# Lattice stage: the sine product moves to VectorE and all eight rows of the normalisation to GpSimd

## What is computed

```
scores = einsum("bhqd,bhkd->bhqk", q, k) / 8
i = int(abs(scores) * 1618);  scores = where(i % 9 in (0, 3, 6), scores / PHI, scores)
attn = softmax(scores)
attn = attn * (sin(C1 * attn) * exp(-attn**2 / PHI) + cos(C2 * attn))
ctx  = einsum("bhqk,bhkd->bhqd", attn, v)
```

## Time and profile before

| | before |
|---|---|
| median of 3 runs | 5878.8 us (5863.97 to 5885.81) |
| the profiled execution | 5868.64 us, of it 5866.9 us span |
| PE busy | 4792.8 us (82%) |
| DVE busy | 4141.1 us (71%) |
| ACT busy | 3988.8 us (68%) |
| POOL busy | 3773.1 us (64%) |
| mean granted TensorE clock | 0.944 of full speed |

### The profile page before, as it was taken

How to read it: one execution, slowest core, us unless ns; L and a number is a source line. 1 busy time by engine, 2 the same in 40 slices (tenths; PEclk the granted TensorE clock), 3 DMA queues, 4 the chain that set the end, 5 groups by cost and what they waited for, 6 DMA issues and landing times. The chain is left out here.

```text
span 5866.9 us, 98280 instructions
## 1 busy us (share of the span) xinstructions
PE 4792.8 (82%) x27646; PEld 2698.8 (46%) x27689; DVE 4141.1 (71%) x7553; ACT 3988.8 (68%) x5466; POOL 3773.1 (64%) x3599
## 2 busy tenths in 40 slices
PE   2688888888888888888888888888888869997899
PEld 1344444444444444444444444444444436554566
DVE  2577777777777777777777777777777656665664
ACT  1577777777777777777777777777777734444332
POOL 4577777777777777777777777777777634443233
PEclk9799999999999999999999999999999879999999
DMA  0000000000000000000000000000000000000000
GB/s 5 23 9 8 8 8 8 8 9 8 10 8 8 8 8 8 8 8 8 9 8 10 8 8 8 8 8 8 8 9 8 4 9 1 2 2 15 3 6 7
DMA packets 34184, 45.24 MB, mean 8 GB/s; under 512 B 24521, under 2 KB 24585, under 8 KB 34058
## 3 DMA queue, kind: packets, MB, share of 16 engines
q1 hardware_dynamic: 32010, 43.49, 2.8%
q0 software_dynamic: 2048, 0.14, 0.1%
HBM read 39.40 MB, written 4.19 MB: 7 GB/s over the span
## 5 line engine op out<-in xcount | busy, mean ns | idle before, releaser
L588 PE MATMUL banks<-ident,att 128*128 128x128 f32 x8192 | 1148.2, 287 | 410.0 <-DVE ag L520 252.1
L588 PEld LDWEIGHTS banks<-ident,att 128*128 128x128 f32 x8192 | 944.6, 147 | 1004.1 <-DVE ag L520 616.9
L630 PE MATMUL banks<-kT,qT 128*128 128x512 f32 x2048 | 1144.8, 658 | 278.9 <-DVE mx L549 269.6
L390 POOL TENSOR_TENSOR sinb<-sinb,ag 128x1024 f32<-128x1024 f32 x512 | 1281.5, 2506 | 85.4 <-ACT sinb L461 70.4
L540 DVE SCALAR_TENSOR_TENSOR mag<-near,mag 128x512 f32<-128x512 int32 x1024 | 857.7, 842 | 483.6 <-POOL near L406 474.2
L400 POOL TENSOR_SCALAR mag<-mag 128x512 f32<-128x512 f32 x1024 | 689.5, 678 | 573.1 <-DVE mag L540 539.0
L647 PE MATMUL outp<-sinb,vo 128*64 128x512 f32 x2048 | 1046.3, 636 | 0.0
L647 PE MATMUL outp<-work,vo 128*64 128x512 f32 x2048 | 1046.3, 636 | 0.0
L406 POOL TENSOR_SCALAR near<-mag 128x512 int32<-128x512 f32 x1024 | 794.0, 775 | 363.9 <-ACT mag L479 300.3
L479 ACT ACTIVATE mag<-banks 128x512 f32<-128x512 f32 x1024 | 599.2, 592 | 283.1 <-PE banks L630 283.0
L497 DVE TENSOR_TENSOR work<-banks,work 128x1024 f32<-128x1024 f32 x512 | 625.1, 1221 | 192.8 <-ACT work L455 189.8
(11 more groups left out here) (198 smaller groups left out, 6357.7 us busy)
## 6 DMA issues: line engine op xcount, KB each, us to landing
x<-xT_dram SPq DMA_DIRECT2D x128, 256.0 KB, 3.5
xT_dram<-xT SPq DMA_DIRECT2D x8, 256.0 KB, 2.9
out<-hres SPq DMA_DIRECT2D x8, 256.0 KB, 2.6
base<-in_L_tok_turns,idx POOLq DMA_INDIRECT x64, 2.3
wqk<-in_L_attn_Wq SPq DMA_DIRECT2D x64, 16.0 KB
wqk<-in_L_attn_Wk SPq DMA_DIRECT2D x64, 16.0 KB
wqk<-in_L_attn_bq SPq DMA_DIRECT2D x64, 0.2 KB
wqk<-in_L_attn_bk SPq DMA_DIRECT2D x64, 0.2 KB
```

Of the source, the lines that this page charges most:

```text
L390: nc.gpsimd.tensor_tensor(sinb[:, k % RING], sinb[:, k % RING], ag[:, k], ALU.mult).then_inc(tmul, 1)
L588: mm = nc.tensor.matmul(turn_pair(k)[:, c, i * P:(i + 1) * P], att[:, p, 4 * half + i, kt * P:(kt + 1) * P], ident[:], is_transpose=True, ...
L630: nc.tensor.matmul(score_bank(n), qT[:, p, (n // 2) * P:(n // 2 + 1) * P], kT[:, p, (n % 2) * 512:(n % 2 + 1) * 512], start=True, stop=Tru ...
```

## The change

The multiplication of sine and gauss term (*product*) is taken from GpSimd's queue and issued by VectorE, behind the turns of the same step and before its keeps and filters. Rows 3 and 7 of the normalisation are taken from VectorE, so GpSimd normalises all eight. The second counter `weights2` goes, and the waits on it: turns and fills now wait for `weights` alone. Tiles, sizes, the step of every operation, ScalarE's and TensorE's queues stay as they are.

```diff
-        DVE_ROWS = (TB // 2 - 1, TB - 1)
@@ gpsimd
-                        if a - P3 in SINE:
-                            k = SINE.index(a - P3)
-                            wait(pool, sined, TB * g + k + 1)
-                            wait(pool, agd, TB * (g + 1))
-                            nc.gpsimd.tensor_tensor(sinb[:, k % RING], sinb[:, k % RING], ag[:, k],
-                                                    ALU.mult).then_inc(tmul, 1)
-                        if a - NORM in EXP and EXP.index(a - NORM) not in DVE_ROWS:
+                        if a - NORM in EXP:
                             j = EXP.index(a - NORM)
                             held(pool, recip, TB * g + j + 1)
                             nc.gpsimd.tensor_scalar(att[:, p, j], att[:, p, j], rs[:, j:j + 1], TURN,
@@ vector
-                        if a - NORM in EXP and EXP.index(a - NORM) in DVE_ROWS:
-                            j = EXP.index(a - NORM)
-                            wait(dve, recip, TB * g + j + 1)
-                            nc.vector.tensor_scalar(att[:, p, j], att[:, p, j], rs[:, j:j + 1], TURN,
-                                                    ALU.mult, ALU.mult).then_inc(weights2, 1)
                         if a - TURNS in EXP:
                             j = EXP.index(a - TURNS)
-                            if j in DVE_ROWS:
-                                wait(dve, weights2, 2 * g + j // 4 + 1)
-                            else:
-                                wait(dve, weights, (TB - 2) * g + j + 1 - j // 4)
                             wait(dve, nned, TB * g)
+                            wait(dve, weights, TB * g + j + 1)
                             nc.vector.tensor_scalar(nturn[:, j], att[:, p, j], ROUND, -ROUND,
                                                     ALU.add, ALU.add).then_inc(turned, 1)
+                        if a - P3 in SINE:
+                            k = SINE.index(a - P3)
+                            wait(dve, sined, TB * g + k + 1)
+                            wait(dve, agd, TB * (g + 1))
+                            nc.vector.tensor_tensor(sinb[:, k % RING], sinb[:, k % RING], ag[:, k],
+                                                    ALU.mult).then_inc(tmul, 1)
@@ tensor, fill
-                wait(pe, weights, (TB - 2) * g + (TB // 2 - 1) * (half + 1))
-                wait(pe, weights2, 2 * g + half + 1)
+                wait(pe, weights, TB * g + TB // 2 * (half + 1))
```

## The result

The changed kernel takes 5881.6 us (median of 20 runs, 5864.0 to 5903.0) against 5859.3 us for the kernel before (20 runs beside it, 5847.7 to 5889.8). The ratio is 1.0037, 95% interval 1.0026 to 1.0049: slower by 0.4%. I had forecast 0.3% faster. Both lie inside "within 0.5%", but the sign is wrong, and there lies the lesson of this case.

The account below looks back on a forecast made before the run. No engine's total sets the time; TensorE, then GpSimd with VectorE, then ScalarE bound each head in turn. Terms 2.35 - 1.15 - 0.9 give 0.3 us a head, 0.25 rounded, 18 us in all: 5861 us, range 5830 to 5895.

Parts of the forecast that it names:

- Parts 1 and 2: Product moves from GpSimd to VectorE at about 1.2 us each; turns 0 starts earlier, gaining 2.35 us a head.
- the walk: Reading one head's engine queues in order of time to price the change: 0.3 us gained a head, 0.25 with rounding.
- (b): Stretch from remove 7 to the first gauss product; TensorE has gaps, GpSimd runs without one, then trades tiles with VectorE.
- Rival A's first half: VectorE's product does not keep GpSimd out, gaining 1.1 us before filter 0; rival A's chance as a whole 0.30.
- Muls 4 and 7 just in time: Before removes 4 and 7: mul 4 ends at 2109.9, mul 7 at 2120.8, both just in time, at no cost.
- Rival B: Products ahead of keep and mul on VectorE make muls 4 and 7 late: 20 to 60 us slower, chance 0.18.
- (a): Stretch from remove 0 to remove 7, where TensorE works nearly without a gap.
- the sum: The terms of one head added: 2.35 - 1.15 - 0.9 = 0.3 us gained, 0.25 with rounding.
- Part 3: Norm 3 on GpSimd: keep 3 comes 7.8 us after turns 0 instead of 6.65, costing 1.15 us a head.
- Part 4: Norm 7 on GpSimd takes 1.62 us and delays fill 4 and ScalarE's square, costing 0.9 us a head.
- (c): Stretch from the first gauss product to the next head's remove 0; ScalarE is full from fill 4's square on.
- Rival C: Lower clock level falls into stretch (a) of every head: 35 us slower, 5896 us, chance 0.08.

Follow-up runs that it names:

- split: Changed kernel with norms 3 and 7 back on VectorE, so only the product moves: 5744.7 us, ratio 0.9809 to the kernel before.
- norm7_lean: lean with norm 7 back on VectorE, norm 3 left on GpSimd: 5792.8 us, ratio 0.9885 to the kernel before.
- split_lean: split with the same waits left out as in lean: 5746.7 us, ratio 0.9807 to the kernel before.
- norms_pool: Kernel before with all eight norms on GpSimd and the product still there: 6057.5 us, ratio 1.0337.
- norm3_lean: lean with norm 3 back on VectorE, norm 7 left on GpSimd: 5851.2 us, ratio 0.9982 to the kernel before.
- lean: Changed kernel with 14 waits a head left out that the first of their kind already covers: 5852.2 us, ratio 0.9991 to the kernel before.
- warm4p: Changed kernel with score 4 done four times and the projection ahead of fill 4 three times: 5845.4 us, ratio 0.997 to the kernel before.

## Why the prediction was right and wrong, step by step

**Parts 1 and 2, gain 2.35 us: right.** Turns 0 starts 7.24 us behind remove 7 on average (7.48 in the heads without the wait at mul 7), where the walk gave 7.3 and the kernel before has 9.7; alone (split) the move takes 2.53 us out of (b), about 2.2 in the heads without that wait. The product's price of 1.2 us was 1.23. The exclusion of the two engines, on which the walk rests, is there with the new product too:

```profile
2054.94 1.67 POOL L399 TENSOR_SCALAR near<-mag 128x512 int32<-128x512 f32 x1 [3.89 <-ACT mag L472]
2057.45 1.50 POOL L399 TENSOR_SCALAR near<-mag 128x512 int32<-128x512 f32 x1 [0.84 <-DVE mag L531]
```

Against these two rounds stand VectorE's products 6 and 7, started at 2054.92 and 2057.25 for 1.22 us each; a round without one takes 0.62 us. Rival A's first half is refuted: VectorE's product does keep GpSimd out. The trace agrees with the rule weighed in the prediction (the Trainium skill, "SBUF — State Buffer", "Who interferes with whom"). So the engines do not meet only at semaphores, as was said at the start: these two also hold each other up without one.

**Muls 4 and 7 just in time: right, with one exception.** Rival B did not come: stretch (a) is not longer at full clock (23.73 against 23.95 us); that it became 0.2 us shorter is in none of the sum's terms. The exception is that remove 7 comes 0.8 us late in every second head, by the wait at mul 7 and not by the product; (b) gives 0.5 us of it back, which leaves 0.1 us a head.

**Part 3, norm 3, cost 1.15 us: right.** It measures 1.12 us from norm7_lean against split_lean, and 1.11 from norms_pool against before.

**Part 4, norm 7, cost 0.9 us: right for the order of work, wrong for what it set off.** Norm 7 took 1.61 us, where the walk gave 1.62, and fill 4 waited for GpSimd 1.97 us in one head and 3.40 us in another; at full clock (c) grew from 23.94 to 24.90 us, 0.96. But the mean (c) grew by 2.18 us, from 24.25 to 26.43: the other 1.2 is the lower level behind fill 4, to which the sum gave nothing. The row of norm 7:

```profile
2082.43 1.61 POOL L388 TENSOR_SCALAR att<-att,rs 128x1024 f32<-128x1024 f32 x1
```

**Rival C, the clock, is the step that failed.** I gave it 0.08 and saw it in one place only: I asked whether the lower level would fall into stretch (a) of every head, as it did of every second one. I did say that the gap before fill 0 would grow from 2.5 to 3.9 us (it grew to 3.49). I did not ask the same of the gap before fill 4, which the walk itself had made 1.2 us longer, nor what lay behind it: matmuls that feed ScalarE at the beginning of its full stretch. There the lower level came, in 42 heads of 62, at 1.3 to 2.9 us each. In the whole head it costs 1.9 us in place of 0.9. The 0.6 us that the new order gains is less than this 1.0 and the 0.1 of the wait at mul 7, and the head is 0.5 us longer: 33 us over 63 heads, less 6 us around them, is the 27 us between the two profiled executions. C's time of 5896 us is by chance that of the profiled execution; its mechanism is right, its place and its chance were wrong. The forecast of 5861 us also stood on 10.2 us between the profiled execution and the median of three runs; with 20 runs the median of before lies 9 us below that execution.

In one sentence: all terms of the sum in the order of work were within about 0.2 us of what was measured, and the term that I had left as a rival was larger than their sum.

**What is shown, and what is not.** Shown: that the lower level falls on fill 4 and scores 7 and 8 in after and that (c) of 42 of 62 heads is over 1 us longer than at full clock, all of them with the lower level in it, where before has 6 such heads and norm7_lean none; and that with norm 7 on GpSimd it lies in (c) whoever does the product (after, norm3_lean, norms_pool). It is no plain rule: lean, with norm 7 on GpSimd, has 19 such heads, and split and split_lean, with it on VectorE, have 17 and 13. Shown too: that filling TensorE's gaps gives time back in after and none in before. Not settled: what decides in which of the heads it comes, and why the wait at mul 7 is 1.6 to 1.9 us in norm7_lean and norm3_lean and 0.4 to 0.9 in the others that have it. In lean 19 heads have it and in after 42, for a difference of 14 waits a head; and most edits that kept it from one place brought some of it to another. I have seen where it falls; a rule for it I haven't.

## What to carry to other kernels

Walk the queues for a change in the order of work, and the terms came out to about 0.2 us here; then ask of every gap of TensorE that the walk makes longer what stands right behind it. If that feeds an engine that is full from there on, price it once at full clock and once at the lower level, and give the second a real chance: here it cost 1.0 us a head against a gain of 0.6. Take a change of several moves apart: the product's move alone was worth 1.9%, and the two norms that came with it cost all of that and more. And before a longer stretch is put down to the clock, look at the granted clock of that very stretch and at the instruction packets: two runs here had a stretch (a) that was 1.8 us longer in every second head at full clock.

## What was not expected of the hardware

- **The lower clock level is a shifting cost.** It was made less in these runs and partly moved, never removed: the mean granted clock went from 0.938 (after) to 0.969 (warm4p), yet the time by 0.7% alone; 0.944 to 0.954 on before was worth nothing. The clock's mean says little here, its place much more.
- **A loop with a few more instructions begins to fetch.** The changed kernel has 201 instruction packets in place of 54 and a wait of 0.6 to 0.9 us at the first VectorE operation behind each of the loop's 29 returns. With 14 waits a head fewer (lean) both are gone, and with one norm back in VectorE's queue (norm7_lean, norm3_lean) both are there again, with a wait of 1.6 to 1.9 us. (The Trainium skill, "Runtime: NRT & Kernel Launch", "Instruction fetch mechanics", states that a taken branch to a place outside the pages held forces a fetch before the engine goes on. The trace agrees in kind.) It came to 0.1 us a head in after and to 0.6 in those two.
- **The excluded operation does not lose the whole length of the other.** The round beside product 6 started 0.02 us behind it and took 1.67 us. In turn, the two would have taken 1.22 + 0.62 = 1.84 us from the product's start; they took 1.69, so 0.15 us of the round lay under the product.
